# An audio block on TensorE: twice normed tokens by a spread ratio, k's levels cleared on GpSimd, another order of the steps

## What is computed

```python
h = dct(frames(x))                                   # [16, 938, 128]
h = h + attn(layernorm(h))
h = h + ffn(layernorm(h))

def attn(x):
    h = layernorm(x, g1, b1);  xx = h shifted by one token
    q, k, v, g = (h * tm + xx * (1 - tm)) @ W        # four mixes, four products
    q, k = exp(rmsnorm(q)), exp(rmsnorm(k));  g = sigmoid(g)
    S, Z = scan of A = lam * A + k v^T, z = lam * z + k, read with q
    x = x + (g * S / Z) @ Wo
    return x + gelu(layernorm(x, g2, b2) @ W1) @ W2

def ffn(xf):                                         # xf is layernorm(h): normed once
    normed = layernorm(xf) * ln_g + ln_b             # normed twice
    x_attn = normed @ attn_w.T + attn_b + xf
    y = gelu(x_attn @ fc1[e] + fc1_b) @ fc2[e] + fc2_b
    return gelu(y @ next_w.T + next_b)
```

## Time and profile before

| what | us |
|---|---|
| median of 3 runs (lowest, highest) | 1095.11 (1094.64, 1097.32) |
| the profiled execution's own time | 1096.16 |
| its span in the trace | 1094.2 |
| TensorE busy | 1058.0 |
| VectorE busy | 919.41 |
| ScalarE busy | 648.01 |
| GpSimd busy | 304.83 |
| mean granted TensorE clock | 0.991 of 2.4 GHz |

### The profile page before, as it was taken

The page is one execution under the profiler, slowest core; times in us unless marked ns, Lnnn a source line. Parts: engine busy times, 40 slices in busy tenths (PEclk is TensorE's granted clock), DMA queues, the critical chain, the costliest instruction groups (busy, mean ns, idle before and its releaser), DMA issues.

```text
span 1094.2 us, 44745 instructions
## 1 busy us (share of the span) xinstructions
PE 1058.0 (97%) x18851; PEld 796.5 (73%) x18851; DVE 919.4 (84%) x2848; ACT 648.0 (59%) x1128; POOL 304.8 (28%) x174
## 2 busy tenths in 40 slices
PE   6679999999999999999999999999999999999997
PEld 6557787786777777777777877777677777777763
DVE  5998988889888888988889898988888888899642
ACT  4346666656765566666566666655576656666533
POOL 4032233242132423313242232324213332331220
PEclk9799999999999999999999999999999999999999
DMA  6232332123323123332212333221332321223210
GB/s 219 88 109 70 97 99 67 53 78 98 98 73 115 54 58 93 97 98 70 83 56 87 98 97 98 71 75 53 97 98 80 102 69 54 89 80 98 80 30 18
DMA packets 51510, 91.55 MB, mean 84 GB/s; under 512 B 9552, under 2 KB 26608, under 8 KB 51312
## 3 DMA queue, kind: packets, MB, share of 16 engines
q1 hardware_dynamic: 51312, 88.69, 26.7%
HBM read 19.50 MB, written 9.78 MB: 27 GB/s over the span
## 4 chain that ended last, share of the span: by engine, by line
PE 93%; DVE 4%; issue 1%; ACT 1%; DMA 1%; SPq 0%; DVEq 0%
PE bank L987 13%; PE bank L1136 11%; PE bank L992 11%; PE bank L1158 10%; PE bank L1129 10%; PE bank L1164 10%; PE bank L1091 7%; PE bank L1066 4%; PE bank L1069 3%; PE bank L1109 3%; PE bank L1074 2%; PE bank L1152 2%; PE bank L1029 2%; PE bank L1113 2%; PE bank L1018 2%
## 5 line engine op out<-in xcount | busy, mean ns | idle before, releaser
L424 POOL TENSOR_TENSOR t_sum<-x,hs 128x512 f32<-128x512 f32 x32 | 40.8, 1276 | 529.9 <-DVE x L795 529.9
L1136 PE MATMUL bank<-w,hid 128*128 128x128 f32 x1024 | 122.7, 278 | 1.5 <-ACT hid L554 1.5
L1158 PE MATMUL bank<-xa,f1w 128*128 128x512 f32 (+1 forms) x256 | 121.1, 570 | 1.9 <-issue 1.8
L574 ACT ACTIVATE hid<-bank,f1b 128x512 f32<-128x512 f32 (+1 forms) x128 | 81.2, 647 | 69.6 <-PE bank L1158 67.7
L1136 PEld LDWEIGHTS bank<-w,hid 128*128 128x128 f32 x1024 | 116.7, 192 | 4.1 <-DVE x L795 1.6
L1129 PE MATMUL bank<-c,w 128*128 128x512 f32 (+1 forms) x256 | 115.8, 565 | 0.9 <-ACT c L548 0.9
L428 POOL TENSOR_TENSOR rr<-vv,nhalf 128x8 f32<-128x8 f32 x32 | 72.3, 2260 | 133.5 <-DVE vv L675 133.5
L1164 PE MATMUL bank<-hid,f2w 128*128 128x512 f32 (+1 forms) x256 | 107.6, 563 | 0.7 <-ACT hid L574 0.7
L1091 PE MATMUL bank<-qx,ki 128*32 128x16 f32 x7680 | 101.0, 193 | 5.7 <-DVE ki L847 5.7
L1091 PEld LDWEIGHTS bank<-qx,ki 128*32 128x32 f32 x7680 | 92.7, 110 | 17.4 <-issue 13.3
L554 ACT ACTIVATE hid<-bank 128x512 f32<-128x512 f32 (+1 forms) x128 | 70.3, 562 | 51.4 <-PE bank L1129 50.4
(11 more groups left out here) (139 smaller groups left out, 2402.9 us busy)
## 6 DMA issues: line engine op xcount, KB each, us to landing
qx<-qq SPq DMA_DIRECT2D x256, 96.0 KB, 2.4
hs<-hs SPq DMA_DIRECT2D x32, 532.0 KB, 3.4
v<-v_f SPq DMA_DIRECT2D x16, 512.0 KB, 3.3
gz<-gate_f SPq DMA_DIRECT2D x16, 512.0 KB, 4.0
xT<-in_xT SPq DMA_DIRECT2D x16, 468.5 KB, 3.5
f1w<-in_fc1T SPq DMA_DIRECT2D x16, 256.0 KB, 3.6
f2w<-g_dram SPq DMA_DIRECT2D x16, 256.0 KB, 3.7
out<-t_sum SPq DMA_DIRECT2D x16, 256.0 KB, 2.4
```

Source lines behind the costliest of these rows:

```text
L1136: last = mm(dst[:, P * i:P * i + P], hid[:, j, P * m:P * m + P], w2[:, j, :], start=(j == 0), stop=(j == 3))
L1158: mm(dst[:, 0:width[g]], f1w[:, P * j:P * j + P], xa[:, cols(g)], start=True, stop=True).then_inc(f1_ok, 1)
```

## The change

The twice normed tokens are no longer made by token and transposed. VectorE makes ra = r1 * v' * r2 per token (v' = v + eps, so that r1 * v' = 1 / r1 and ra = r2 / r1), SyncE stores the 512 numbers of a half to DRAM in token order (`hand_ratio`) and loads them back as one row spread over all 128 partitions (`spread_ratio`) into ra_f, which takes x2's place. GpSimd multiplies xa by it into c1 (`nms`). ln_g is folded into the weight (wat_g) and ln_b @ attn_w into the bias (at_c) once at the start. n2s, nmTs and nb3 are gone. GpSimd clears ki, ko and kw. All five lists and `USES` are new; dct0, dct1, nT0 and nT1 now take three banks, so `spare` has three.

```diff
@@ new tiles
-        nb3 = sb("nb3", TILES)
-        h1, n1, n2 = t_sum, nl2, x2
+        h1, n1 = t_sum, nl2
+        ra, ra_f = sb("ra", TILES), x2[:, :, :].rearrange("p m n -> p (m n)")
+        ra_dram = nc.dram_tensor("ra_dram", [2, HALF], F32, kind="Internal").ap()
+        wat_g, at_c = sb("wat_g", P), sb("at_c", 1)
@@ SyncE
+            def hand_ratio(b, g):
...
+                sp.wait_ge(ra_ok, there)
+                sp.dma_start(ra_dram[g, :].rearrange("(m p) -> p m", p=P), ra[:, four(g)], allow_slow_non_contiguous=True).then_inc(rd_in[g], 16)
+
+            def spread_ratio(b, g):
...
+                sp.wait_ge(rd_in[g], there)
+                sp.dma_start(ra_f[:, HALF * g:HALF * g + HALF], ra_dram[g:g + 1, :].to_broadcast([P, HALF])).then_inc(rb_in[g], 16)
@@ GpSimd
+            gp.memset(ko[:, :, :], 0.0)
+            gp.memset(kw[:, :, :], 0.0).then_inc(s_lvo, 1)
             gp.wait_ge(s_init, 2)
...
             def pow1(b):
...
+                if first(b):
+                    gp.memset(ki[:, :, :], 0.0).then_inc(s_lev, 1)
...
+            def nms(b, g):
+                gp.wait_ge(xc_ok, nth(b, 2, g + 1))
+                gp.wait_ge(rb_in[g], nth(b, 16, 16))
+                gp.wait_ge(w1_ok, nth(b, 8, 4 * g + 4))
+                gp.tensor_tensor(c1[:, cols(g)], xa[:, cols(g)], ra_f[:, cols(g)], ALU.mult).then_inc(nm_ok, 1)
@@ ScalarE
+                nc.scalar.activation(at_c[:, :], spare[E % len(spare)][:, E:E + 1], ACT.Identity, bias=col("at_b")).then_inc(s_gc, 1)
+                nc.scalar.activation(wat_g[:, :], wat[:, :], ACT.Copy, scale=col("f_g")).then_inc(s_gc, 2)
...
             def attn_in(b):
                 act.wait_ge(hs2_in, nth(b, 16, 16))
-                before(act, nmT_ok, b, 2, 2)
+                before(act, nm_ok, b, 2, 2)
@@ VectorE
+            def ratio(b, g):
+
+                dve.wait_ge(r3_ok, nth(b, 2, g + 1))
+                before(dve, rd_in[g], b, 16, 16)
+                V.tensor_tensor(ra[:, four(g)], rr3[:, four(g), 0], vv3[:, four(g), 0], ALU.mult).then_inc(rm_ok, 1)
+                dve.wait_ge(rm_ok, nth(b, 2, g + 1))
+                V.tensor_tensor(ra[:, four(g)], ra[:, four(g)], rr3[:, four(g), 1], ALU.mult).then_inc(ra_ok, 1)
@@ TensorE
+                mm(spare[E % len(spare)][:, E:E + 1], wat[:, :], col("f_b"), start=True, stop=True).then_inc(s_gp, 1)
...
-                mm(dst[:, 0:width[g]], wat[:, :], c1[:, cols(g)], start=True, stop=True).then_inc(at_ok, 1)
+                mm(dst[:, 0:width[g]], wat_g[:, :], c1[:, cols(g)], start=True, stop=True).then_inc(at_ok, 1)
```

More of the change, by code:

```diff
@@ L378, in body @@
                 if (b := at(3)) is not None:
+                    expert(b)
+                if (b := at(1)) is not None:
+                    hand_h1(b)
+                if (b := at(3)) is not None:
+                    hand_ratio(b, 1)
+                if (b := at(2)) is not None:
+                    spread(b, 2)
+                if (b := at(3)) is not None:
+                    spread_ratio(b, 1)
+                if (b := at(2)) is not None:
+                    spread(b, 3); hand_gate(b)
+                if (b := at(3)) is not None:
+                    store(b, 0)
+                if (b := at(1)) is not None:
+                    spread(b, 0)
+                if (b := at(3)) is not None:
                     store(b, 1)
                 if (b := at(1)) is not None:
-                    hand_h1(b)
+                    hand_v(b); spread(b, 1); hand_h2(b)
+                if (b := at(2)) is not None:
+                    hand_ratio(b, 0); spread_ratio(b, 0)
             every_round(body)
@@ L431, in body @@
             def body(at):
+                if (b := at(2)) is not None:
+                    states(b)
+                if (b := at(3)) is not None:
+                    nms(b, 1)
+                if (b := at(1)) is not None:
+                    powq(b, 0)
+                if (b := at(2)) is not None:
+                    pow2(b, 0)
+                if (b := at(1)) is not None:
+                    powq(b, 1)
+                if (b := at(2)) is not None:
+                    resid(b, 0); resid(b, 1); pow2(b, 1); pow3(b, 0)
                 if (b := at(0)) is not None:
@@ L554, in gelu1 @@
                 nc.scalar.activation(hid[:, j, cols(g)], bk(f"w1_{g}{j}")[:, 0:width[g]], ACT.Gelu).then_inc(ge1, 1)
-            def n2s(b, g):
-                act.wait_ge(nb3_ok, nth(b, 2, g + 1))
-                for m in tiles(g):
-                    last = nc.scalar.activation(n2[:, m, :], h1[:, m, :], ACT.Identity, scale=rr3[:, m, 1:2], bias=nb3[:, m:m + 1])
-                last.then_inc(n2_ok, 1)
             def xas(b, g):
@@ L1172, in body @@
             def body(at):
+                if (b := at(0)) is not None:
+                    dcts(b, 0)
                 if (b := at(2)) is not None:
-                    pairs_a(b, 6); pairs_b(b, 6); scan(b, 5)
+                    attends(b, 0)
+                if (b := at(1)) is not None:
+                    qkv(b, "k", 0)
+                if (b := at(3)) is not None:
+                    f1s(b, 1, 3)
+                if (b := at(2)) is not None:
+                    pairs_a(b, 5); scan(b, 4); pairs_b(b, 5)
+                if (b := at(1)) is not None:
+                    qkv(b, "k", 1)
+                if (b := at(3)) is not None:
+                    oTs(b, 0); f2s(b, 1)
                 if (b := at(1)) is not None:
@@ L1203, in body @@
                 if (b := at(1)) is not None:
-                    gates(b, 0)
+                    pairs_b(b, 0); pairs_a(b, 1)
                 if (b := at(2)) is not None:
@@ L1207, in body @@
                 if (b := at(1)) is not None:
-                    pairs_a(b, 1); pairs_b(b, 1)
+                    zts(b)
                 if (b := at(2)) is not None:
```

321 lines of the change are left out of this document (145 added, 176 removed), and 10 rows, old and new, of the table USES.

## The result

The changed kernel takes 1363.89 us (median of 4 runs, 1353.99 to 1365.58) against 1095.3: a ratio of 1.2428, with a 95% interval of 1.2395 to 1.2461. The forecast was 1083.0, the range 1075 to 1099.

The account below looks back on a forecast made before the run. TensorE bounds the kernel, busy for 962.97 of 964 us in steady rounds. Span: 1094.2 - 14.1 - 2.4 + 2.1 + 1.0 + 1.3 = 1082.1; + 1.96 - 1.05 gives 1083.0 us, range 1075 to 1099.

Parts of the forecast that it names:

- the store's price: Ratio's store to DRAM, each steady round: taken as 2.3 us, between bounds of 1.8 and 4.4.
- the part on the new dependence: Steady rounds, chain from stats3 to ats: store and spread may take 6.1 us together before TensorE waits; 5.1 assumed, cost 0.
- the rival's own rule: Late transfers in steady rounds: each microsecond beyond 6.1 for store and spread together costs 16 us.
- the fill: Start of the kernel: k at about 35, round three near 75.1, 2.1 us later, plus 1.0 for work at 1.2 GHz.
- rival 1: Steady rounds: the two transfers are late, 1101 us at 7.2 together, 1126 at 8.8; chance 0.20, 0.11 of it slower.
- 1.4 us to spare: Steady rounds, second half: TensorE gives 15 us from w2s(1) to ats(1), leaving the chain there 1.4 us of slack.
- The steady rounds: From 86 to 1050 us: transposes save 14.1 us and fewer narrow-to-wide changes 2.4; period 63.7 us for 64.7.
- nothing stands late: Steady rounds: VectorE and ScalarE stay covered by TensorE's work, zero waits from round four on.
- twice 0.16: Steady rounds, new dependence: VectorE's two ratio operations, with the wait between them, estimated at 0.4 us.
- GpSimd does them while it would wait anyway: Start of the kernel: memsets of ki, ko, kw take GpSimd 5.7 us in its waiting time and spare VectorE 7.0.
- the drain: Last 44 us: 10.9 us without TensorE work against 9.6 before, +1.3.
- The sign that I named: In the trace: store and spread above 6.1 us together, with TensorE waiting for GpSimd's c 16 times.

Follow-up runs that it names:

- without transfers and with the gate first: Changed kernel without the ratio's store and spread (nobody waits, ratio left out), VectorE's second gate operation ahead of the second half's ratio: 1082.83 us, 0.9888 of the kernel before.

## Why the prediction was wrong, point by point

**The step that failed** is the store's price in the part on the new dependence: "for the store I take 2.3", and 4.4 as its upper bound. It took 8.6 to 11.2, 8.8 in the round shown. The spread was priced too low as well, 2.8 for a median of 5.1. The store's bound came from f1b's 1024 pieces of 16 bytes, and was taken as one for a number of pieces: 512 pieces of 4 bytes take 8.8 us, 128 of 16 bytes 1.4 to 3.4. f1b is moreover a read of DRAM; no row had a write of small pieces, and I said so and still gave the bound a ceiling. With the measured 8.8 + 5.1 = 13.9 the rival's own rule gives 1083 + 16 x 7.8 = 1208. The Trainium skill's sentence that I had set beside this rival (DMA: Bandwidth & Descriptors, section Rules for kernel authors: one descriptor per element for a strided last dimension) agrees with the packets under 512 B: 17408 more than before, of which 32 x 512 = 16384 are these.

**What no case had** is the rest, 156 us. I priced a transfer by who waits for it. A 4-byte store holds TensorE up with nobody waiting (+111 in the new order, +52 in the old), and each wait at ats takes TensorE's clock down with it, some 4.7 us per round by my estimate, which I had counted in the fill and not in rival 1. And the rule had one wait per round. There are two, 4.97 and 4.85 us in the round shown, since the second half, to which I gave 1.4 us to spare, waits too; there nms itself is often longer, 1.84 us in the mean for a shortest of 1.08.

**The steady rounds.** Eight transposes less and the order's changes: I had 63.7 for the period, without transfers and with the gate first it is 63.3, and TensorE's busy time falls by 1058.0 - 1039.2 = 18.8 for my 16.5. Right, a little small. That nothing stands late was wrong by 1.0 us per round. I had the rule on shared interfaces before me and set it aside because resid keeps its length in all 32 cases. It does; but the length of one GpSimd operation beside the VectorE work of the old order doesn't tell what VectorE pays, nor what nms pays elsewhere. VectorE's ratio is held, from 0.16 to 2.45 us, and "twice 0.16" was a price for an idle GpSimd; nms is held where VectorE comes first. A slip without effect: of the 36.2 us without TensorE work I put all outside 86 to 1050, where 35.2 of them lie.

**The fill.** k behind the second batch's samples: right (VectorE waited 9.57, I had 11.0). Not seen: the memset beside the normalisations, 2.9 us at the head of all; the folded stores and the samples behind them move with it. q's product waits 0.99 us for wat_g, which I had put at no price. k came at 38.66 for my 35, round three's first product at 81.95 for 75.1. "GpSimd does them while it would wait anyway" counted GpSimd's time and not VectorE's beside it, so 7.0 us of gain by themselves gave 0.4.

**The sum.** The kernel without transfers and with the gate first takes 1082.83, the forecast was 1083.0. That is partly luck. Against the span before: TensorE's busy time -18.8 (mine -16.5), idle time in the steady rounds +1.5 (mine 0), in the fill +5.7 (mine +2.1, and 1.0 for the clock), in the drain -1.6 (mine +1.3). Two errors of mine met.

**The chances.** 0.12 for the side that came true, and a range that ended at 1099, because rival 1 was cut off at a bound from a row of another kind. The sign that I named (over 6.1 together, TensorE's waits for nms's c) is what the trace shows, with 32 waits where I had named 16.

## What to carry to other kernels

Look at the innermost run of every new small DMA: the same 2 KB cost 8.8 us and the engines' time in 4-byte pieces, and nothing in 16-byte pieces that nobody waits for. Reorder the data on the reading side if need be; here that cost GpSimd 0.3 us per product. A transfer that the old trace doesn't show, with someone waiting for it in every round, has no upper bound from rows of another kind; measure it idle in the old kernel first. And work handed to GpSimd isn't free when VectorE's queue has an SBUF operation at that moment: whichever comes second can stand until the other is done, and behind a run of short VectorE operations without a gap GpSimd stood until the last. Ask what both do then, and shift the work by the length of one operation.

## What the runs showed of the hardware that was not expected

- Writes of 4-byte pieces to DRAM pause TensorE where it has its shortest instructions (64 matmuls in some 0.75 us), up to 4.5 us at a time, and nothing in the trace releases the pause. In the changed kernel VectorE too stands for 72.5 us at the copies of px (L818) without a releaser; before it was 1.8. While such stores run, the 16 KB packets that bring instructions take up to 4.0 us in the old order and 5.0 in the changed kernel, for at most 1.6 before. Whether late instructions are the pauses is open, since in half of the pause time or more no such packet is under way.
- The hold-up differed with the order: 3.5 us per store in the new one, 1.6 in the old. What makes the difference isn't shown.
- A VectorE operation on 128x4 with two SBUF inputs took 2.45 us beside a GpSimd product, 0.16 without; eight 128x128 normalisations with one SBUF input took 5.02 beside a memset, 2.13 without. The first gate operation, which reads PSUM, kept its 0.68 beside pow3 and the start of that product.
- GpSimd is held too, when VectorE comes first: nms took up to 3.9 us, for 1.5, beside a run of VectorE operations with two SBUF inputs.
- nms with one input at a step of 16 bytes took a median of 1.55 us and at the least 1.52, for 1.26 with both inputs contiguous.
